# Six loads for a group's operand stacks instead of seven, two of them reading one block several times, and half of them moved behind another load in the queue

## The chip, the cores and the metric

The kernel runs on one core of a Trainium2 chip. The metric is device time in microseconds for one execution. TensorE does the matrix products, VectorE (DVE) and ScalarE (ACT) read their results, GpSimd (POOL) does small arithmetic on the side, and SyncE (SP) issues every DMA of this kernel, one after the other, as a queue written by hand. The data of a DMA are moved by 16 DMA engines that all transfers of the core share.

## The reference: what is computed

Cross attention with 32 heads of size 16 over four batches of 512 rows, and after it a feed-forward block with quantised activations and ternary weights. Cut to the part that the change touches:

```python
q = (layernorm(x) @ Wq).reshape(b, n, 32, 16)
k, v = jnp.split(ctx @ Wkv, 2, axis=-1)
q, k = apply_axial_rope(q, pos_map), apply_axial_rope(k, ctx_pos_map)
w = jax.nn.softmax(jnp.einsum("bqhd,bkhd->bhqk", q, k) / 4.0, axis=-1)
attn = jnp.einsum("bhqk,bkhd->bqhd", w, v).reshape(b, n, 512)
x = x + attn @ Wout + bout
x = x + ffn(layernorm(x), w_fc, w_proj)      # bitlinear, gelu, bitlinear
```

## The kernel before, in words

Three stages follow one another. In the first (to about 147 us) `Project` normalises, projects and rotates q and k, and splits each float32 value into three bf16 parts (0 is the coarse one, 2 the finest), which are stored in DRAM as `q_parts` and `k_parts`. In the second (147 to about 512 us) `Attend` works on 32 groups, each four heads of one batch. The third is the feed-forward block.

A product of q and k to nearly float32 precision is the sum of six products of parts. The kernel gets them in one matmul: it stacks six parts of q on 96 partitions (`q_stack`, six blocks of 16) and six parts of k on 96 partitions (`k_stack`), so that the contraction over 96 rows adds up six pairs. Each stack has four slots; group g uses slot g mod 4. `load_stacks` fills both from DRAM: a block of 16 partitions holds 4096 bytes in each, so a block is 64 KB, a stack 384 KB, and a group 768 KB.

TensorE's order is `tensor_step(s)`, for s = 2 to 34. Step s computes for group s the scores of which only the row maxima are kept (`scores`, L667, eight pairs of matmuls with `j` = 0 to 7, read by DVE at L740), for group s-2 the transposed scores less their maxima (`scores_turned`, L692, 16 matmuls, read by ACT's exponential at L760), and the product with v (`weigh_v`, L706). A step begins with one `scores_turned` matmul and then the first pair of `scores`. The maxima enter the transposed scores as two more rows of `q_stack` (98 rows in all), and they come there by a chain over engines: after the last L740 of a group, POOL negates and splits the maxima (`split_maxima`, L771 to L777), SP turns them with a DMA transpose (`turn_max`, L592), waits for that, and loads the result into the two rows (`load_max`, L596). So what is computed for group g in step g is used in step g+2, and one step lies between.

SP's order in iteration s of the attention loop, before:

```python
att.turn_max(sp, s - 2)       # waits for split_ready of group s-2
att.load_stacks(sp, s)        # 3 loads of q, 4 of k, for s = 4 to 31
att.load_max(sp, s - 2)       # waits for the turned maxima
att.load_weight(sp, w_fc, w_proj, s)
att.pack_sums(sp, s)          # store_sums; load_sums and store_inverse if s is even, load_quotients if odd
att.turn_weight(sp, s - 2)
```

`load_quotients` (odd s from 9 on) brings 256 KB of numerators (L638) and 256 KB of inverse sums (L639). Its source and its destination for each are these: 128 partitions of 2048 bytes in SBUF, and in DRAM a pattern whose outermost count is 8 heads with 16 rows inside (for the inverse sums the same row 16 times).

Of the kernel before, what the change touches and what calls it, by code (L numbers as in the profile page):

```python
# [15 lines left out]
BATCH, SEQ, DIM, CTX = 4, 512, 512, 256  # L16
HEADS, HEAD = 32, 16
# [4 lines left out]
GH = 4  # L22
HG = HEADS // GH
GROUPS = BATCH * HG
# [12 lines left out]
DMA = 16  # L37
PAIR_STORES = DMA * 2 * 2 * PARTS
STACK_SLOTS = 4
STACK_LOADS = DMA * 7  # L40
INPUT_SLOTS = 4
QUARTERS = FFN // DIM
O_SLOTS = 2
# [5 lines left out]
def need(eng, semaphore, value):  # L49

    if value > 0:
        eng.wait_ge(semaphore, value)
# [457 lines left out]
class Attend:  # L510
# [59 lines left out]

    def load_stacks(self, sp, g):
        mem, slot = self.mem, g % STACK_SLOTS
        for pair in range(2):
            sp.wait_ge(self.prj.parts_stored[pair], PAIR_STORES * (g // HG + 1))
        need(sp, self.st_ready, (g - STACK_SLOTS + 1) * 16)
        for stack_sb, where, runs in (
            (mem.q_stack, mem.q_parts, ((0, 0, 3), (3, 0, 2), (5, 0, 1))),
            (mem.k_stack, mem.k_parts, ((0, 1, 1), (1, 0, 1), (2, 0, 1), (3, 0, 3))),  # L580
        ):
            src = where[g].rearrange("t (d h) c -> (t d) (h c)", h=GH)
            for to, part, count in runs:
                sp.dma_start(stack_sb[to * HEAD:(to + count) * HEAD, slot].rearrange("p h c -> p (h c)"),  # L584
                             src[part * HEAD:(part + count) * HEAD]).then_inc(self.stacks_loaded[slot], DMA)

    def turn_max(self, sp, g):
        sp.wait_ge(self.split_ready, g + 1)
# [65 lines left out]
    def scores(self, pe, g, j):  # L654
        head, slot = j // 2, g % STACK_SLOTS
        if j == 0:
            pe.wait_ge(self.stacks_loaded[slot], (g // STACK_SLOTS + 1) * STACK_LOADS)
        if g == self.EARLY and j == 0:
# [13 lines left out]
    def early_scores(self, pe, i):  # L672

        g, head, c = i // (GH * CHUNKS), i // CHUNKS % GH, i % CHUNKS
        if i % (GH * CHUNKS) == 0:
            pe.wait_ge(self.stacks_loaded[g], STACK_LOADS)
        need(pe, self.early_read, i)
# [482 lines left out]
def xattn_ffn(nc, x, ctx, pos, wq, wkv, wout, bout, w_fc, w_proj, out):  # L1160
    with ExitStack() as stack:
# [3 lines left out]
        mem = Memory(nc, stack)  # L1165
        prj = Project(nc, mem, sem)
        att = Attend(nc, mem, prj, sem)
# [5 lines left out]
        @block.sync  # L1173
        def _(sp):
            prj.load_first(sp, x, ctx, pos, wq, wkv)
            prj.set_rows(sp, att.rows_set)
            prj.load_ctx(sp, ctx, 2)
            prj.load_x(sp, x, 2)
            for s in range(TILES + 6):
                if 3 <= s + 1 < TILES:  # L1180
                    prj.load_ctx(sp, ctx, s + 1)
                    prj.load_x(sp, x, s + 1)
                if within(s - 2, TILES):
                    prj.load_piece(sp, w_fc, w_proj, s - 2)
                if s == TILES + 4:
                    sp.wait_ge(prj.projected[1], TILES)
                    att.load_weight(sp, w_fc, w_proj, 0)
                    att.load_weight(sp, w_fc, w_proj, 1)
                if within(s - 5, TILES) and (s - 5) % 2 == 1:
                    prj.store_parts(sp, s - 5)  # L1190
                if s in (8, 10, 13, 15):
                    att.load_stacks(sp, (8, 10, 13, 15).index(s))
                if s == TILES + 3:
                    att.turn_max(sp, 0)
                    att.load_max(sp, 0)
            for pair in range(2):
                sp.wait_ge(prj.parts_stored[pair], PAIR_STORES * BATCH)

            for s in range(GROUPS + 3):
                if 1 <= s - 2 < GROUPS:  # L1200
                    att.turn_max(sp, s - 2)
                if STACK_SLOTS <= s < GROUPS:
                    att.load_stacks(sp, s)
                if 1 <= s - 2 < GROUPS:
                    att.load_max(sp, s - 2)
                if 2 <= s < GROUPS:
                    att.load_weight(sp, w_fc, w_proj, s)
                att.pack_sums(sp, s)
                if within(s - 2, GROUPS):
                    att.turn_weight(sp, s - 2)  # L1210
                if s == GROUPS - 7:
                    rows.load_bias(sp, bout)
                if GROUPS - 6 <= s < GROUPS - 2:
                    rows.load_weight(sp, wout, s - GROUPS + 6)
                if GROUPS - 2 <= s < GROUPS:
                    rows.load_x(sp, x, s - GROUPS + 2)
            rows.load_x(sp, x, 2)
            rows.turn_u(sp, 0)
            rows.load_x(sp, x, 3)
            rows.turn_u(sp, 1)  # L1220

            for s in range(TILES + 3):
                if s + 4 < TILES:
                    rows.load_x(sp, x, s + 4)
                if within(s - 1, TILES - 1):
                    rows.turn_h(sp, s - 1, 0)
                if s + 2 < TILES:
                    rows.turn_u(sp, s + 2)
                if within(s - 1, TILES - 1):
                    rows.turn_h(sp, s - 1, 1)  # L1230
                if s == TILES:
                    for part, half in ((0, 0), (0, 1), (1, 0), (1, 1)):
                        rows.turn_last(sp, part, half)
                if within(s - 3, TILES):
                    rows.store(sp, out, s - 3)
                if s < 6:
                    att.pack_sums(sp, GROUPS + 3 + s)
            for i in range(2):
                sp.wait_ge(rows.out_stored[i], TILES // 2 * DMA)
# [295 lines left out]
```

## Time and profile before

| | |
|---|---|
| time, median of 3 runs | 794.77 us (794.23 to 797.53) |
| the profiled execution's own time | 797.79 us |
| its span, first to last instruction | 795.9 us |
| PE busy | 768.5 us, 97% |
| DVE busy | 674.4 us, 85% |
| ACT busy | 456.1 us, 57% |
| DMA queue of SP, share of 16 engines | 65.7% |

The span leaves 1.9 us of the profiled execution outside the first and last instruction. PE is matmul, PEld the weight load that overlaps it, SPq is SP's own queue of DMA issues. A busy PE means that matmuls were in flight, not that TensorE was at its peak.

### The profile page before, as it was taken

To read this page: it belongs to the slowest core of one execution; us is meant where nothing else is said; L and a number is where in the kernel's file an instruction comes from. 1 tells how busy PE (TensorE), PEld (TensorE's weight loads), DVE (VectorE), ACT (ScalarE), POOL (GpSimd) and SP (SyncE) were. 2 spreads that over 40 slices of the span, in tenths; PEclk is the share of its full clock that TensorE was granted. 3 is DMA by queue.
4 is the path that set the end of the run, shared out by engine and by line. 5 is a ranking of instruction groups with operands and counts; after the bars stand their busy time and mean duration, and the time that the engine had idled before them with its cause. 6 is when DMAs were issued, how large, how long until landed. Compare 5 with 4: busy or idle time off the path is not lost.

```text
span 795.9 us, 11662 instructions
## 1 busy us (share of the span) xinstructions
PE 768.5 (97%) x3812; PEld 331.6 (42%) x3812; DVE 674.4 (85%) x945; ACT 456.1 (57%) x811; POOL 341.0 (43%) x445
## 2 busy tenths in 40 slices
PE   4899999799999999999999999999999999999998
PEld 3688877233333222323322222244444444444443
DVE  7788998688888888888888888269999999898895
ACT  5677776477777777767777777734322333223430
POOL 4688777743454455445445544623222121110001
PEclk9999999699999999999999999999999999999999
DMA  8488897535577769796887996326456654555545
GB/s 288 127 216 241 256 254 184 129 109 137 147 141 152 154 158 142 152 171 149 146 155 180 171 176 137 82 57 137 107 110 144 132 106 93 108 117 87 112 87 137
DMA packets 178861, 117.22 MB, mean 147 GB/s; under 512 B 119746, under 2 KB 150514, under 8 KB 178802
## 3 DMA queue, kind: packets, MB, share of 16 engines
q1 hardware_dynamic: 178802, 116.49, 65.7%
q8 instruction: 30, 0.49, 0.3%
q14 instruction: 29, 0.24, 0.1%
HBM read 64.50 MB, written 25.43 MB: 113 GB/s over the span
## 4 chain that ended last, share of the span: by engine, by line
PE 86%; DMA 6%; DVE 3%; SPq 2%; POOL 1%; issue 1%; ACT 1%; POOLq 0%; ACTq 0%
PE banks L967 14%; PE banks L952 14%; PE banks L706 13%; PE banks L692 12%; PE banks L281 11%; PE banks L667 11%; PE banks L938 7%; DMA stack_words<-max_rows 4%; DMA max_rows<-max_parts 2%; PE banks L310 2%; SPq L584 1%; PE banks L678 1%; DVE maxima L740 1%; DMA attn_words<-in_x_dram 1%; ACT probs_words L760 1%
## 5 line engine op out<-in xcount | busy, mean ns | idle before, releaser
L760 ACT ACTIVATE probs_words<-banks 128x512 f32<-128x512 f32 x512 | 272.1, 598 | 101.7 <-PE banks L692 101.0
L740 DVE TENSOR_REDUCE maxima<-banks 128x2 f32<-128x1024 f32 x240 | 283.4, 1216 | 45.6 <-PE banks L667 45.5
L692 PE MATMUL banks<-stack_words 98*128 98x512 bf16 x512 | 175.4, 386 | 4.8 <-DMA stack_words<-max_rows 3.4
L667 PE MATMUL banks<-stack_words 96*128 96x512 bf16 x480 | 144.9, 383 | 0.0
L706 PE MATMUL banks<-probs_words,late_words 128*32 128x512 f32 x1024 | 137.3, 608 | 0.7
L952 PE MATMUL banks<-ternary_words,late_words 128*128 128x512 f16 x512 | 113.1, 380 | 0.0
L967 PE MATMUL banks<-ternary_words,stack_words 128*128 128x512 f16 x512 | 112.9, 380 | 0.0
L1130 ACT ACTIVATE probs_words<-probs_words,h_moments 128x2048 f32<-128x2048 f32 (+1 forms) x17 | 32.2, 1901 | 135.4 <-DVE h_moments L1027 135.4
L692 PEld LDWEIGHTS banks<-stack_words 98*128 98x128 bf16 x512 | 39.8, 98 | 150.0 <-ACT probs_words L760 109.9
L771 POOL TENSOR_SCALAR neg_max<-maxima 128x16 f32<-128x16 f32 x32 | 8.3, 258 | 163.0 <-DVE maxima L740 161.2
L967 PEld LDWEIGHTS banks<-ternary_words,stack_words 128*128 128x128 f16 x512 | 49.9, 98 | 64.4 <-issue 6.6
L952 PEld LDWEIGHTS banks<-ternary_words,late_words 128*128 128x128 f16 x512 | 50.0, 98 | 61.5 <-issue 1.7
L1153 POOL TENSOR_SCALAR h_powers<-h_moments 128x1 f32<-128x1 f32 x16 | 5.5, 342 | 153.4 <-DVE h_moments L1027 153.4
L667 PEld LDWEIGHTS banks<-stack_words 96*128 96x128 bf16 x480 | 47.4, 99 | 56.7 <-issue 1.9
L1124 ACT ACTIVATE probs_words<-banks,row_scale 128x512 f32<-128x512 f32 x64 | 42.3, 682 | 27.5 <-PE banks L952 27.5
L938 PE MATMUL banks<-v_words,attn_words 128*128 128x512 f32 x128 | 57.7, 593 | 0.0
L786 POOL TENSOR_SCALAR late_words<-late_words,limits 128x512 f16<-128x512 f32 x32 | 50.1, 1566 | 0.3 <-POOL late_words L791 0.2
L788 POOL TENSOR_SCALAR late_words<-late_words,limits 128x512 f16<-128x512 f32 x32 | 50.2, 1570 | 0.0
L506 POOL TENSOR_TENSOR ternary_words<-attn_words,ternary_words 128x512 bf16<-128x512 f32 x32 | 37.3, 1166 | 24.3 <-ACT ternary_words L471 23.5
L706 PEld LDWEIGHTS banks<-probs_words,late_words 128*32 128x32 f32 x1024 | 20.2, 108 | 54.9 <-ACT probs_words L760 50.3
L502 POOL TENSOR_TENSOR attn_words<-attn_words 128x512 f32<-128x512 f32 x32 | 41.2, 1290 | 2.2 <-DVE attn_words L396 2.0
L1022 DVE BATCH_NORM_STATS2 h_stats<-probs_words 128x6 f32<-128x512 f32 x64 | 39.4, 679 | 0.0
(139 smaller groups left out, 962.5 us busy)
## 6 DMA issues: line engine op xcount, KB each, us to landing
o_rows<-late_words SPq DMA_DIRECT2D x32, 256.0 KB, 3.3
k_parts<-ternary_words SPq DMA_DIRECT2D x48, 128.0 KB, 3.2
q_parts<-ternary_words SPq DMA_DIRECT2D x48, 128.0 KB, 2.5
stack_words<-q_parts SPq DMA_DIRECT2D x32, 192.0 KB, 3.1
stack_words<-k_parts SPq DMA_DIRECT2D x96, 64.0 KB, 2.7
stack_words<-k_parts SPq DMA_DIRECT2D x32, 192.0 KB, 2.7
attn_words<-in_x_dram SPq DMA_DIRECT2D x16, 256.0 KB, 4.4
probs_words<-in_L_ffn_w_fc_dram SPq DMA_DIRECT2D x16, 256.0 KB, 3.7
```

The lines of the kernel that those rows point to most:

```text
L281: mm = self.nc.tensor.matmul(out, lhs[a][:, slot, k * P:(k + 1) * P], rhs[b][:, k, :], start=(a + b + k == 0), stop=(a == 1 and k == count ...
L667: mm = self.nc.tensor.matmul(self.score_slot[j % 2][:, i], self.mem.q_stack[0:STACK, slot, head, c * P:(c + 1) * P], self.mem.k_stack[0:ST ...
L692: self.nc.tensor.matmul(self.st_bank[(g * 16 + k) % self.ST_BANKS], self.mem.k_stack[0:STACK + 2, slot, head, c * P:(c + 1) * P], self.mem ...
L706: mm = self.nc.tensor.matmul(self.pv_bank[32 * j:32 * j + 32], self.v_ones[:, g % 2, c, j, :], self.probs[:, c, j, :], start=(c == 0), sto ...
L740: dve.tensor_reduce(self.maxima[:, g % 2, 2 * j:2 * j + 2], self.score_slot[j % 2], AX.X, ALU.max).then_inc(self.scores_read, 1)
L760: act.activation(self.probs[:, c, head, :], self.st_bank[(g * 16 + k) % self.ST_BANKS], ACT.Exp, scale=1 / math.sqrt(HEAD)).then_inc(self. ...
L786: pool.tensor_scalar(self.below[:], self.raw[:, w], limits[:, 1, w:w + 1], None, ALU.is_lt).then_inc(self.cut, 1)
L788: pool.tensor_scalar(self.ternary[:, w], self.raw[:, w], limits[:, 0, w:w + 1], None, ALU.is_gt).then_inc(self.cut, 1)
L938: mm = self.nc.tensor.matmul(self.y_bank[n % 2], att.attnT[:, n // CHUNKS * KX + k, c * P:(c + 1) * P], self.wout_sb[:, k, :], start=(k == ...
L952: mm = self.nc.tensor.matmul(self.fc_bank[o], self.uT[:, n % U_SLOTS, part * KX + k], self.fcT[:, k, o], start=(k + part == 0), stop=(k == ...
L967: mm = self.nc.tensor.matmul(self.proj_bank[r], self.hT[:, r, part, k], self.projT[:, k // 2, k % 2], start=(k + part == 0), stop=(part == ...
L1124: act.activation(self.h[:, n % H_SLOTS, o * DIM:(o + 1) * DIM], self.fc_bank[o], ACT.Gelu, scale=self.row_scale[:, n % U_SLOTS]).then_inc( ...
```

## The change

The six pairs of parts are the same six products in another order. The q stack holds parts 0,1,2,0,1,0 before and after. The k stack held 1,0,0,0,1,2 and holds 0,0,0,1,1,2 now. The four loads of k (three of one block, one of three blocks) become three: part 0 three times, part 1 twice, part 2 once. The first two read their one block of DRAM with an added outermost step of zero, counts 3 and 2, and write 48 and 32 partitions. In SP's attention loop the loads of q stay ahead of the load of the maxima, and those of k go behind it. The bytes moved are the same.

```diff
-STACK_LOADS = DMA * 7
+STACK_LOADS = DMA * 6
...
+    def load_q(self, sp, g):
...
+        src = self.mem.q_parts[g].rearrange("t (d h) c -> (t d) (h c)", h=GH)
+        for to, count in ((0, 3), (3, 2), (5, 1)):
+            sp.dma_start(self.mem.q_stack[to * HEAD:(to + count) * HEAD, slot].rearrange("p h c -> p (h c)"),
+                         src[0:count * HEAD]).then_inc(self.stacks_loaded[slot], DMA)
+
+    def load_k(self, sp, g):
+        slot = g % STACK_SLOTS
+        for part, to, count in ((0, 0, 3), (1, 3, 2), (2, 5, 1)):
+            src = self.mem.k_parts[g, part].rearrange("(d h) c -> d (h c)", h=GH)
+            sp.dma_start(self.mem.k_stack[to * HEAD:(to + count) * HEAD, slot].rearrange("p h c -> p (h c)"),
+                         src.unsqueeze(0).to_broadcast([count, HEAD, GH * SEQ])).then_inc(self.stacks_loaded[slot], DMA)
...
                 if STACK_SLOTS <= s < GROUPS:
-                    att.load_stacks(sp, s)
+                    att.load_q(sp, s)
                 if 1 <= s - 2 < GROUPS:
                     att.load_max(sp, s - 2)
+                if STACK_SLOTS <= s < GROUPS:
+                    att.load_k(sp, s)
```

SP's queue in one odd iteration of the attention loop, before: `max_rows` are the turned maxima, `max_parts` the maxima before it, `late_words` holds the raw weight, the quotients' operands and the ternary weight.

```order
L592 DMA_TRANSPOSE max_rows<-max_parts 128x128 [waits max_loaded_1,max_padded,split_ready]
L584 DMA stack_words<-q_parts 48x2048 [waits st_ready,parts_stored_1,parts_stored_0]
L584 DMA stack_words<-q_parts 32x2048
L584 DMA stack_words<-q_parts 16x2048
L584 DMA stack_words<-k_parts 16x2048 x3
L584 DMA stack_words<-k_parts 48x2048
L596 DMA stack_words<-max_rows 2x16x128 [waits max_turned_1]
L606 DMA late_words<-in_L_ffn_w_proj_dram 128x2x256 [waits ternary_ready]
L617 DMA o_rows<-late_words 128x512 [waits o_saved]
L638 DMA late_words<-o_rows 128x1x512 [waits inverse_stored_0]
L639 DMA late_words<-inverse_rows 128x1x512
L612 DMA_TRANSPOSE ternary_words<-late_words 128x4x128 [waits ternary_ready]
```

The same iteration of the changed kernel, in its own line numbers, from the maxima's transpose to the ternary weight's:

```order
L599 DMA_TRANSPOSE max_rows<-max_parts 128x128 [waits max_loaded_1,max_padded,split_ready]
L580 DMA stack_words<-q_parts 48x2048 [waits st_ready,parts_stored_1,parts_stored_0]
L580 DMA stack_words<-q_parts 32x2048
L580 DMA stack_words<-q_parts 16x2048
L603 DMA stack_words<-max_rows 2x16x128 [waits max_turned_1]
L587 DMA stack_words<-k_parts 48x1x2048
L587 DMA stack_words<-k_parts 32x1x2048
L587 DMA stack_words<-k_parts 16x2048
L613 DMA late_words<-in_L_ffn_w_proj_dram 128x2x256 [waits ternary_ready]
L624 DMA o_rows<-late_words 128x512 [waits o_saved]
L645 DMA late_words<-o_rows 128x1x512 [waits inverse_stored_0]
L646 DMA late_words<-inverse_rows 128x1x512
```

The load of the maxima moved ahead of four loads of k, and three loads of k now stand behind its wait; all that follows them (weights, sums, quotients) kept its order. The two broadcast loads have the same printed form as L638 and L639, a destination of partitions by one by a row. The order of TensorE, DVE, ACT and POOL is the same as before, instruction by instruction.

## Rows read from the trace of the kernel before

**Rows 1.** The page: span, granted clock by slice, and the chain that ended last.
```profile
span 795.9 us, 11662 instructions
...
PEclk9999999699999999999999999999999999999999
...
PE 86%; DMA 6%; DVE 3%; SPq 2%; POOL 1%; issue 1%; ACT 1%; POOLq 0%; ACTq 0%
```

**Rows 2.** Waits in the attention stage, 147 to 512 us: total, times, longest.
```profile
PEld banks L692 <- DMA stack_words<-max_rows: 7.8, 10, 1.6
...
PE banks L692 <- DMA stack_words<-max_rows: 3.4, 6, 1.1
...
SPq L592 <- POOL max_parts L777: 64.0, 30, 4.2
```

**Rows 3.** Chain that ended last, 296 to 335 us: start, duration, what.
```profile
298.25 0.45 PE banks L667 x2
...
298.72 1.24 DVE maxima L740
...
301.03 5.18 DMA max_rows<-max_parts
...
306.23 4.77 DMA stack_words<-max_rows
...
311.05 0.39 PE banks L692
```

**Rows 4.** Timeline of SP, 300 to 350 us: start, duration, issue.
```profile
302.30 1.44 SPq L584 DMA_DIRECT2D stack_words<-q_parts  x3
303.78 1.81 SPq L584 DMA_DIRECT2D stack_words<-k_parts  x4
306.23 0.71 SPq L596 DMA_DIRECT2D stack_words<-max_rows  x1
306.99 0.41 SPq L603 DMA_DIRECT2D late_words<-in_L_ffn_w_fc_dram  x1
...
324.92 1.12 SPq L592 DMA_TRANSPOSE max_rows<-max_parts  x1
...
336.27 1.12 SPq L592 DMA_TRANSPOSE max_rows<-max_parts  x1
```

**Rows 5.** Stretches of half a microsecond; the last two columns are DMA share and GB/s.
```profile
300.50:301.00 0.50, 0.50 (x7) 0.26 (x4) 0.50 (x2) 0.10 (x1) 0.42 (x3) 1.00 0.45 143
301.00:301.50 0.50, 0.50 (x4) 0.21 (x3) 0.50 (x2) 0.50 (x2) 0.50 (x2) 1.00 0.45 172
...
304.00:304.50 0.50, 0.50 (x4) 0.26 (x3) 0.11 (x1) 0.50 (x2) 0.42 (x2) 1.00 0.06 25
...
308.00:308.50 0.50, 0.50 (x9) 0.14 (x8) 0.50 (x2) 0.50 (x2) 0.00 (x0) 1.00 1.08 131
```

**Rows 6.** DMA issues of 301 to 312 us, an iteration of even s: KB each, us to landing.
```profile
stack_words<-q_parts SPq DMA_DIRECT2D x1, 192.0 KB, 5.0
stack_words<-k_parts SPq DMA_DIRECT2D x3, 64.0 KB, 5.3
...
ternary_words<-late_words SPq DMA_TRANSPOSE x1, 3.6
```

**Rows 7.** The same of 312.3 to 324 us, an iteration of odd s.
```profile
stack_words<-k_parts SPq DMA_DIRECT2D x3, 64.0 KB, 3.3
...
max_rows<-max_parts SPq DMA_TRANSPOSE x1, 2.2
...
ternary_words<-late_words SPq DMA_TRANSPOSE x1, 6.1
```

**Rows 8.** All that touches `stack_words`: duration min/median/max in ns, and its landings.
```profile
L584 SPq DMA_DIRECT2D stack_words<-k_parts x128: 407/420/1629, 63.6 to 479.4; - x128
...
DMA to landing us min/median/max: 2.1/3.2/5.5
```

**Rows 9.** Busy time in the attention stage; clock, DMA share and GB/s end the row.
```profile
147.00:500.00 353.00, 349.00 (x1937) 104.28 (x1938) 304.14 (x289) 258.51 (x486) 181.24 (x231) 0.99 0.72 148
```

More of the change, by code:

```diff
@@ L569, in __init__ @@
         self.divided = sem("divided")
-    def load_stacks(self, sp, g):
-        mem, slot = self.mem, g % STACK_SLOTS
+    def load_q(self, sp, g):
+        slot = g % STACK_SLOTS
         for pair in range(2):
@@ L577, in load_stacks @@
         need(sp, self.st_ready, (g - STACK_SLOTS + 1) * 16)
[L578 to L585, printed above, removed]
+        src = self.mem.q_parts[g].rearrange("t (d h) c -> (t d) (h c)", h=GH)
[3 more added lines that the diff above has]
+    def load_k(self, sp, g):
+        slot = g % STACK_SLOTS
+        for part, to, count in ((0, 0, 3), (1, 3, 2), (2, 5, 1)):
+            src = self.mem.k_parts[g, part].rearrange("(d h) c -> d (h c)", h=GH)
+            sp.dma_start(self.mem.k_stack[to * HEAD:(to + count) * HEAD, slot].rearrange("p h c -> p (h c)"),
+                         src.unsqueeze(0).to_broadcast([count, HEAD, GH * SEQ])).then_inc(self.stacks_loaded[slot], DMA)
+    def load_stacks(self, sp, g):
+        self.load_q(sp, g)
+        self.load_k(sp, g)
     def turn_max(self, sp, g):
```

## The prediction

> **What bounds the kernel now.** I read the page first, for its chain of work that ended last: 86% of it is TensorE, at a granted clock of nearly one throughout, and 6% is DMA [rows 1]. So the kernel is bound by TensorE, with small holes, and a change of DMAs can win at most those holes. Next the waits of the attention stage, to see how large they are: TensorE waited for the load of the maxima 7.8 us in its weight loads and 3.4 us in its matmuls, 11.2 us in all [rows 2]. It shows no wait for the q and k stacks. In the whole stage, TensorE was busy 349 of 353 us [rows 9]. SP is no bound: it waited 64 us for POOL's split maxima [rows 2].
>
> Then the chain in time, at one of the holes [rows 3]. The last matmuls of a step's scores end at 298.70. DVE and POOL take until 301.03, when SP issues the transpose of the maxima; it lands 5.18 us later, at 306.21. The load of the maxima is issued at 306.23, lands 4.77 us later, and TensorE goes on at 311.05. Steps without a hole are 11.35 us apart (336.27 - 324.92, [rows 4]). A chain therefore begins at the end of one step and is needed one step later. I call L its length, here 311.05 - 298.70 = 12.35 us. If L exceeds 11.35 us the excess is a hole, 1.0 us here. A hole also gives the next step's chain more room, because its chain started before the hole and its need comes after it. So over a pair of steps the holes add up to the excess of the slower of the two chains, not to the sum of both. Before: 14 pairs with 1.0 us are 14 us, against the 11.2 us seen, which bears the reckoning out.
>
> **The load of the maxima moved forward.** Before, it stood behind 3 + 4 stack issues of 1.44 + 1.81 us [rows 4], and its two partitions wait in the DMA engines behind all 768 KB of stacks. Four of those seven issues and half the bytes go behind it. In the step shown the issue was not late because of SP (the k issues ended at 305.59, the transpose landed at 306.21), but the landing was: 4.77 us for 8 KB. With 384 KB ahead instead of 768 KB, at the 131 GB/s at which the stack loads ran [rows 5], it lands 384/131 = 2.9 us sooner. L for the maxima falls to about 9.4 us, below 11.35. All 11.2 us of present holes go: -11.2 us. That is the gain, and its bound. The issue saved (0.42 us, [rows 8]) is worth nothing while SP waits 64 us for POOL.
>
> **The loads of k moved back.** They are issued after the maxima's load: at 306.99 instead of 303.78 in this step, since SP stands in its wait for the transpose. Behind them stand the weight load, the store of the sums, the quotients and the ternary transpose; all are slid back by 1.4 us or so, less than SP's average slack of 64/30 = 2.1 us, so I cost them at nothing. The k stack is needed at the second matmul group of the step, 0.22 us after its start. By [rows 6] the old k loads landed 5.3 us after issue, the last issue at about 305.1, so at 310.4, while the step could begin at 298.70 + 11.35 = 310.05 and wants the stack at 310.27. They had no room already, and the maxima's hole hid it: this cover is used up by the move.
>
> **The loads of k with a repeated block.** This term decides. The rows show one kind of transfer with a short outermost count, the quotients, whose count is 8. They are the last large transfers of an odd iteration, so I read the stretch just before the next transpose of maxima as theirs. There the DMA share stands at 0.45, which is 7.2 of 16 engines, at 143 to 172 GB/s, so 20 to 24 GB/s for each engine; and where the queue has nearly run dry one engine alone shows as a share of 0.06 with 25 GB/s [rows 5]. The stack loads of the other form reach all engines, a share of 1.08 [rows 5]. The ternary transpose, queued behind the quotients in odd iterations, landed in 6.1 us instead of 3.6 [rows 6, 7]. So a leading count of 8 gave 8 engines. I take it that leading counts of 3 and 2 give 3 and 2 engines. Then one engine carries 16 rows of 4096 bytes of the first load, 16 of the second and one of the third: 33 x 4096 = 135 KB, where it carried 6 x 4096 = 25 KB. At 25 GB/s that is 5.4 us, at 143/7.2 = 19.9 GB/s it is 6.8 us. To it comes the smallest landing of a stack load, 2.1 us [rows 8], which I take for what does not grow with size.
>
> The rows alone don't exclude that counts of 3 and 2 are spread in another way, by the 48 and 32 partitions of the destination, for instance. A rule of the Trainium skill bears on it, in DMA: Bandwidth & Descriptors, section "Why a DMA increments its semaphore by 16 and not by 1": the number of engines is the largest one, up to 16, that divides the slowest count above one of both sides; its "Rules for kernel authors" warn of just this leading broadcast. By the rule the sum is the one below; by a spread over all 16 it would be the first rival's. The trace agrees with the rule at the count of 8 and has no case of 3 or 2.
>
> **The sum.** L for the k stack in the changed kernel, from the end of a step's scores: 2.33 to the transpose's issue [rows 3]; the transpose's landing; 0.78 to the first k issue (0.02 + 0.71 + 0.05, [rows 4]); 2.1 fixed; the transfer; less 0.22, since it is needed that much after the step's start.
> The landing of the transpose is between 2.2 us [rows 7] and 5.18 us [rows 3]. It is 5.18 where the quotients still fill eight engines. Now the k loads add 4.7 us or so of work to two of these engines, while the hole gives them time to drain. I take 4.6, nearer the slow row.
> - Low: 2.33 + 2.2 + 0.78 + 2.1 + 5.4 - 0.22 = 12.6 us, excess 1.25 us a pair.
> - Taken: 2.33 + 4.6 + 0.78 + 2.1 + 5.4 - 0.22 = 15.0 us, excess 3.65 us a pair.
> - High: 2.33 + 5.18 + 0.78 + 2.1 + 6.8 - 0.22 = 17.0 us, excess 5.65 us a pair.
>
> Stacks are loaded in 28 iterations (s = 4 to 31), 14 pairs: 17, 51 and 79 us of holes. They replace the present 11.2: +6, +40, +68 us. The four groups that are loaded in the projection stage are loaded long before use; there I cost the crowding of two engines at nothing, since the inputs are loaded tiles ahead, with an upper bound of 4 x 2 = 8 us if such cover is gone. The feed-forward stage is the same and only starts later. Against the profiled execution (797.79 us, span 795.9) this gives 838 us; it stood 3.0 us above the median of 794.77, so against the median **835 us**, 5% slower.
>
> **Rivals.** *The repeated blocks are spread over all 16 engines* (the other side). For it: the rows have no count of 3 or 2, and the destination is 48 partitions. Against it: the share of 0.45 at a count of 8. Then the maxima's holes of 11.2 us go, but the k stack, whose data are issued 1.4 us or so later, lands between 310.4 as now and 311.1, that is 0.1 to 0.8 us late in every pair: 14 x 0.1 to 14 x 0.8 = 1 to 11 us of holes in place of 11.2. So 0 to -10 us, 785 to 795, about 790. It decides if the k loads land within 4 us of their issue. Chance 0.10, of which 0.07 is faster by over 0.5% (4 us, about what a measurement of this kernel can tell from no change).
>
> *Few engines, but the hole is covered.* If the transposes land in 2.2 us in all steps, and the narrow loads overlap with what is now waiting, the excess falls to the 0.8 us a pair that equals the present holes: about 795, within 0.5%. For it: 12.6 us is near 11.35. Against: three of the terms would have to be at or below their least row. Chance 0.06.
>
> *The two crowded engines become the bound.* Bytes of a pair of steps on the busiest engine: mean 148 GB/s x 22.7 us / 16 = 210 KB; 32 KB more because the quotients use half the engines; less 49 KB of old k, plus 270 KB of new: 463 KB. At 25 GB/s that takes 18.5 us and at 19.9 GB/s 23.3, under the forecast's pair of 26.4. From 17.5 GB/s down it decides. The stack loads ran at 131/16 = 8 GB/s for each engine when all ran at once [rows 5], so lower rates exist, though likely of something that all share. At 15 GB/s a pair is 30.9 us, 8.2 x 14 - 11 = +104 us: 899 us. Chance 0.06.
>
> **How the numbers follow.** The forecast has 0.78. Faster by over 0.5%: 0.07 (most of the first rival). Within 0.5%: 0.03 + 0.06 = 0.09. Slower: 0.78 + 0.06 = 0.84. The range reaches from the covered case (795, less 2 for what runs differ by) to the high sum (794.77 + 68 = 863) with the projection's bound (8), 3 more because the pairs are alike only roughly: 793 to 874. It leaves out most of the first rival and the third, about 0.16. The forecast's own range is 801 to 863.
>
> **What would show it.** If right: TensorE's wait for the maxima is gone; a new wait stands at the first scores of a step (before L667's matmuls) for k's loads, 2 to 6 us in every second step or shared between both; k's loads of 192 KB and 128 KB land in 7 us and more, and stretches with a DMA share of 0.12 to 0.2 at 50 to 75 GB/s appear. If wrong: k's loads land in 2 to 4 us. TensorE's clock was at 1.00 where the present holes are; a fall with the longer holes would add to the time, and is in no term. Most of the error I expect in the landing of the transpose, behind two crowded engines.

## The result, and the profile after

The changed kernel takes 881.78 us (median of 6 runs, 877.27 to 883.33), the kernel before 796.85 us in the same count of runs (794.23 to 798.62). The ratio is 1.106, with a 95% interval of 1.103 to 1.110: some 85 us slower, where 835 us was forecast and 874 us was the upper end of the range. All numbers below are of the faster of the chip's two states; one execution of one experiment (896.12 us, the kernel with small quotients and no fillers) fell in the slower state and is left out.

First the page of the changed kernel: span, granted clock by slice, and the chain that ended last.

```profile
span 880.0 us, 11630 instructions
...
PEclk9999998999999899978999788999999999999999
...
PE 66%; DMA 15%; SPq 9%; DVE 4%; issue 2%; POOL 2%; ACT 1%; POOLq 0%; DVEq 0%; ACTq 0%
```

Against [rows 1] the span has grown by 84.1 us, TensorE's share of the chain has fallen from 86% to 66%, DMA's has risen from 6% to 15%, and the clock shows sevens and eights in the middle, where the attention stage lies. Where the time went is told by the waits of that stage (147 to 600 us; total, times, longest), which answer to [rows 2]:

```profile
PEld banks L674 <- DMA stack_words<-k_parts: 55.6, 16, 4.2
PE banks L674 <- DMA stack_words<-k_parts: 47.7, 15, 3.7
...
PE banks L699 <- DMA stack_words<-max_rows: 1.1, 1, 1.1
```

L674 is the `scores` matmul (L667 before), L699 the transposed one (L692 before). The wait for the maxima is gone but for one; a wait for k of about 3.2 us stands at 15 steps, one in each of the 14 pairs and one more behind the last. It shows twice, once for the weight load and once for the matmul behind it: these are the same holes. The chain in time through one of them answers to [rows 3]:

```profile
332.98 0.45 PE banks L674 x2
...
333.45 1.24 DVE maxima L747
...
338.47 0.74 SPq L603
...
339.25 0.74 SPq L587
...
340.69 7.80 DMA stack_words<-k_parts
...
348.54 0.99 PE banks L674 x2
```

From the end of the scores (333.43) to the landing of k (348.49) it is 15.06 us. The first k load is issued at 339.25 and all of k has landed 9.24 us later; before, a k load of such an iteration landed 5.3 us after its issue [rows 6]. The timeline of SP, which answers to [rows 4], gives the length of a pair of steps:

```profile
335.77 1.11 SPq L599 DMA_TRANSPOSE max_rows<-max_parts  x1
...
347.11 1.11 SPq L599 DMA_TRANSPOSE max_rows<-max_parts  x1
...
363.78 1.11 SPq L599 DMA_TRANSPOSE max_rows<-max_parts  x1
```

One step is 11.34 us as ever, the other 16.67: the pair takes 28.01 us. Stretches of half a microsecond around the hole (TensorE first, clock, DMA share and GB/s last), to set beside [rows 5]:

```profile
346.00:346.50 0.50, 0.00 (x0) 0.00 (x0) 0.02 (x1) 0.00 (x0) 0.26 (x1) 1.00 0.18 74
...
347.50:348.00 0.50, 0.00 (x0) 0.00 (x0) 0.00 (x0) 0.00 (x0) 0.50 (x1) 1.00 0.13 49
...
349.00:349.50 0.50, 0.50 (x3) 0.05 (x1) 0.00 (x0) 0.00 (x0) 0.50 (x1) 0.50 0.25 26
...
351.50:352.00 0.50, 0.50 (x5) 0.13 (x2) 0.04 (x1) 0.00 (x0) 0.08 (x1) 0.50 0.95 131
352.00:352.50 0.50, 0.50 (x3) 0.20 (x2) 0.50 (x1) 0.19 (x1) 0.32 (x1) 0.96 0.67 131
```

Two things are to be seen. While TensorE waits, the DMA share is 0.18 at 74 GB/s and then 0.13 at 49 GB/s: three engines of sixteen, then two, each at about 25 GB/s. (Of the other five half microseconds of this hole one has 0.20 at 66 GB/s. In the other four, with shares of 0.80 to 5.88, other transfers are mixed in.) And from the end of the hole to 352 us TensorE runs at 0.50, its 1.2 GHz level. In the trace before, the clock was at 1.00 from 156 to 500 us, its holes included.

The attention stage as a whole, from its first transposed scores to the first matmul of the next stage, before and after (TensorE's busy time is the first number behind the length):

```profile
147.57:505.53 357.96, 353.38 (x1961) 105.02 (x1962) 304.07 (x288) 262.66 (x495) 186.36 (x235) 0.99 0.72 148
```

```profile
152.93:589.67 436.74, 386.79 (x1961) 107.77 (x1962) 307.55 (x288) 264.26 (x495) 186.93 (x235) 0.91 0.76 122
```

The stage grew by 78.8 us. TensorE took 33.4 us longer over the same matmuls, at a mean clock of 0.91 instead of 0.99, and stood idle for 45.4 us more.

### The profile page after: what moved, and what is told of

Same layout as the page of the kernel before. It is cut to its first block, busy times and chain, and to the rows that moved or that the text cites. A ratio compares the mean times of both kernels' runs of the same rounds, so it can differ in the third digit from the quotient of the medians.

```text
span 880.0 us, 11630 instructions
## 1 busy us (share of the span) xinstructions
PE 803.5 (91%) x3812; PEld 335.8 (38%) x3812; DVE 678.9 (77%) x945; ACT 457.5 (52%) x811; POOL 340.8 (39%) x445
## 4 chain that ended last, share of the span: by engine, by line
PE 66%; DMA 15%; SPq 9%; DVE 4%; issue 2%; POOL 2%; ACT 1%; POOLq 0%; DVEq 0%; ACTq 0%
PE banks L974 13%; PE banks L959 13%; DMA stack_words<-k_parts 12%; PE banks L713 10%; PE banks L699 8%; PE banks L674 8%; PE banks L281 7%; PE banks L945 6%; SPq L587 2%; DVE maxima L747 2%; SPq L580 2%; SPq L599 2%; PE banks L310 1%; SPq L603 1%; SPq L243 1%
## 5 line engine op out<-in xcount | busy, mean ns | idle before, releaser
L674 PE MATMUL banks<-stack_words 96*128 96x512 bf16 x480 | 155.1, 406 | 47.7 <-DMA stack_words<-k_parts 47.7
L699 PE MATMUL banks<-stack_words 98*128 98x512 bf16 x512 | 184.8, 405 | 2.5 <-ACT probs_words L767 1.3
L713 PE MATMUL banks<-probs_words,late_words 128*32 128x512 f32 x1024 | 150.9, 664 | 0.7
L699 PEld LDWEIGHTS banks<-stack_words 98*128 98x128 bf16 x512 | 41.1, 100 | 161.7 <-ACT probs_words L767 98.4
L674 PEld LDWEIGHTS banks<-stack_words 96*128 96x128 bf16 x480 | 48.0, 103 | 115.2 <-DMA stack_words<-k_parts 55.6
```

What stands on the lines that cost most here:

```text
L674: mm = self.nc.tensor.matmul(self.score_slot[j % 2][:, i], self.mem.q_stack[0:STACK, slot, head, c * P:(c + 1) * P], self.mem.k_stack[0:ST ...
L699: self.nc.tensor.matmul(self.st_bank[(g * 16 + k) % self.ST_BANKS], self.mem.k_stack[0:STACK + 2, slot, head, c * P:(c + 1) * P], self.mem ...
L713: mm = self.nc.tensor.matmul(self.pv_bank[32 * j:32 * j + 32], self.v_ones[:, g % 2, c, j, :], self.probs[:, c, j, :], start=(c == 0), sto ...
```

## The experiments

Times are medians with the ratio to the kernel before, run on the same chip, and its 95% interval.

**The place in the queue alone.** Seven loads of the old form, k behind the maxima.

```diff
-STACK_LOADS = DMA * 6
+STACK_LOADS = DMA * 7
...
+        src = self.mem.k_parts[g].rearrange("t (d h) c -> (t d) (h c)", h=GH)
+        for to, part, count in ((0, 1, 1), (1, 0, 1), (2, 0, 1), (3, 0, 3)):
+            sp.dma_start(self.mem.k_stack[to * HEAD:(to + count) * HEAD, slot].rearrange("p h c -> p (h c)"),
+                         src[part * HEAD:(part + count) * HEAD]).then_inc(self.stacks_loaded[slot], DMA)
```

> Only the place in the queue is changed: seven loads of the old form (every one on a source of 16 or 48 rows), q ahead of the maxima's load, k behind it. Theory (the broadcast loads sit on 3 and 2 of the 16 DMA engines, and all of the loss comes from that): no hole over 1 us at a step's start, TensorE's clock stays at about 0.99, and the time is that of the kernel before or a few us less: 786 to 798 us. Rival (the place behind the maxima's load, 3.2 us later, makes k late): a wait for k_parts in every second step as in the changed kernel, 3 us or more, and 840 to 885 us.

797.17 us, ratio 1.001 (0.9985 to 1.0035): no change. Its waits show why there was no gain either:

```profile
PE banks L674 <- DMA stack_words<-k_parts: 1.1, 2, 0.6
...
PE banks L699 <- DMA stack_words<-max_rows: 0.3, 1, 0.3
```

The maxima are hardly waited for any more, and what is left is a short wait for k. So with loads of the old form the move is harmless and worth nothing that can be measured; the loss is not from the place alone.

**The form alone.** Six loads with the leading broadcasts, all ahead of the maxima's load.

```diff
-                    att.load_q(sp, s)
+                    att.load_stacks(sp, s)
...
-                if STACK_SLOTS <= s < GROUPS:
-                    att.load_k(sp, s)
```

> Only the form is changed: six loads with the two leading broadcasts, all ahead of the maxima's load as before. Theory (narrow loads are the cost): the chain now ends with the maxima's load, which waits on the same crowded engines behind k; L is shorter than in the changed kernel because k is issued about 3 us earlier, so holes of 2 to 5 us a pair: 830 to 885 us. Rival (the place is the cost, the form costs nothing): 790 to 800 us.

869.08 us, ratio 1.090 (1.0855 to 1.0951). The form alone carries 72 us of the loss. The place, which costs nothing with the old form, adds some 13 us to the narrow one. The wait has changed its name, since the maxima's two rows now queue behind the narrow loads:

```profile
PE banks L699 <- DMA stack_words<-max_rows: 40.7, 14, 3.5
```

**The same repetition with an outermost count of 16.** Rows of a block are interleaved in the stacks, for q and k alike, so that the copies are the inner count.

```diff
-        src = self.mem.q_parts[g].rearrange("t (d h) c -> (t d) (h c)", h=GH)
+        src = self.mem.q_parts[g].rearrange("t (d h) c -> d t (h c)", h=GH)
...
-                         src[0:count * HEAD])
+                         src[:, 0:count])
...
-                         src.unsqueeze(0).to_broadcast([count, HEAD, GH * SEQ]))
+                         src.unsqueeze(1).to_broadcast([HEAD, count, GH * SEQ]))
```

> Queue order and number of loads (six) as in the changed kernel, same bytes; the rows of a block are interleaved in the stacks (partition d x count + copy), so that the outermost count of every source is 16 and the repetition is the inner one. The six products are the same. Theory (outermost count sets the number of engines): k lands in 2.5 to 4.5 us, no holes over 1 us, clock about 0.99, 785 to 797 us. Rival (reading one block of DRAM several times, or the step of zero itself, is slow): as the changed kernel, 860 to 885 us.

801.37 us, ratio 1.005 (1.0028 to 1.0074). The same bytes from the same blocks with the same step of zero, in the same order and number of loads, lose 4 us instead of 85. Issues of its stretch 301 to 313 us (KB, us to landing):

```profile
stack_words<-k_parts SPq DMA_DIRECT2D x1, 192.0 KB, 3.3
...
stack_words<-k_parts SPq DMA_DIRECT2D x1, 128.0 KB, 3.2
```

So it is the outermost count, not the reading of one block three times. The time lies 4 us above the theory's band: this kernel still waits 7.5 us for k, in nine steps. The cured form thus gains nothing over the kernel before either.

**Half the dose.** Part 0 in three loads of 16 rows; only part 1 keeps its leading broadcast of 2. The busiest engine has 20 rows a group instead of 33.

```diff
-STACK_LOADS = DMA * 6
+STACK_LOADS = DMA * 8
...
-        for part, to, count in ((0, 0, 3), (1, 3, 2), (2, 5, 1)):
+        for part, to, count in ((0, 0, 1), (0, 1, 1), (0, 2, 1), (1, 3, 2), (2, 5, 1)):
```

> The changed kernel with part 0 of k in three loads of 64 KB (16 rows each, outermost count 16) in place of one with a leading broadcast of 3; part 1 keeps its leading broadcast of 2. The busiest engine has 3 + 16 + 1 = 20 rows of k a group instead of 33. Theory (time follows the rows on the busiest engine, 5.3 us a pair of steps for 27 rows more than before's 6): 14 rows more than before's 6 give about half of the loss, 835 to 850 us. Rival (only the broadcast of 3 matters, or the number of issues): 795 to 805 us or 875 to 885 us.

838.55 us, ratio 1.054 (1.050 to 1.057), +43 us. For 14 rows more than before on the busiest engine that is 3.1 us a row; the changed kernel has 27 rows more and 85 us, 3.1 us a row too. At these two doses the loss is in proportion to the rows on the busiest engine, inside the theory's band. Its parts are not: in the attention stage TensorE's matmuls took 11.3 us longer than before (33.4 in the changed kernel) and its idle time grew by 26.1 us (45.4). So the straight line is a sum of two parts that bend, and no law to go by at other doses.

**Keeping TensorE busy in the hole.** Twelve extra matmuls, whose results are overwritten, fill part of the hole.

```diff
+        if j == 0 and g >= 6 and g % 2 == 0:
+            need(pe, self.scores_read, (g - self.EARLY) * 2 * GH - 1)
+            for i in range(12):
+                self.nc.tensor.matmul(self.score_slot[0][:, i % 2], ...)
         if j == 0:
             pe.wait_ge(self.stacks_loaded[slot], (g // STACK_SLOTS + 1) * STACK_LOADS)
```

> The changed kernel with 12 more matmuls (96 rows x 512 columns, 2.6 us at the full clock, results overwritten) on TensorE ahead of its wait for the stacks, in the 13 steps of even s from 6 on, where its holes are. Theory (each hole of 3.5 us is followed by 3.4 us at a granted clock of 0.5, which costs 1.7 us more): the holes that are left are under 1.5 us, the clock in the attention stage is 0.99 or so, and the time falls by 13 x 1.7 = 22 us or a little more, to 852 to 862 us, though more work is done. Rival (the clock in these stretches costs nothing, since TensorE waits anyway): 880 us or more.

878.57 us, ratio 1.100 (1.095 to 1.104), with a mean clock of 0.977 instead of 0.948. The time fell by 3 us, not by 22. In the attention stage the clock rose from 0.91 to 0.97. TensorE was busy 399.55 of 434.27 us there, of which the 13 groups of fillers are 13 x 2.75 = 36 us, so its own matmuls took 10 us longer than before the change instead of 33: the clock did give back some 23 us. But fillers and idle time together are 70.5 us, where the changed kernel idled for 50, and that took 20 of the 23 us away again. Part of it shows in the chain:

```profile
334.30 4.05 DMA max_rows<-max_parts
...
361.98 5.37 DMA max_rows<-max_parts
```

The maxima's transpose now lands in 4.1 and 5.4 us, where the changed kernel's load of the maxima could be issued 2.70 and 2.88 us after it (median landing of all 32 transposes: 4.0 us against 2.7). In the changed kernel 16.67 us lie between the transpose of the odd iteration and the next one, here 14.98, so the engines have less time to drain. That this is why the transpose is slower is argued, not shown.

**The quotients taken off the crowded engines**, with the fillers and without them. Both kernels leave out most of the numerators and inverse sums.

```diff
+        if pair < 2:
             sp.dma_start(self.numer[:, r], rows[0]).then_inc(self.inverse_loaded[r], DMA)
...
+        else:
+            for now in (self.numer, self.inverse):
+                sp.dma_start(now[0:HEAD, r], rows[0][0]).then_inc(self.inverse_loaded[r], DMA)
```

> The kernel with the 12 filling matmuls in even steps, and with the two quotient loads of every pair of groups from the third on cut from 256 KB (8 engines, 64 KB on each) to 32 KB (16 rows); it leaves out the numerators and inverse sums of those pairs. With the fillers the transpose of the maxima landed in 4.1 to 5.4 us and ate up what the clock gave back. Theory (the backlog of the two crowded engines, to which the quotients belong, sets that landing): it falls to under 3 us, a pair of steps to about 26 us, and the time by some 12 x 2 = 24 us, to 850 to 860 us. Rival (the two narrow k loads alone set the pair, whatever else is queued): 875 us or more.

> The changed kernel without fillers, with the quotient loads cut in the same way; it leaves out the same data. In the changed kernel the transpose ahead of the long hole already lands in under 3 us, since a hole and a slow stretch give the engines time to drain. Theory (the chain of an even step, 2.3 us to the transpose, 2.7 for it, 0.8, and 9.2 for k, sets the pair together with the half clock after the hole): little changes, 870 to 882 us. Rival (the sum of all work on the busiest engine sets the pair): 64 KB less at 25 GB/s is 2.6 us a pair, 845 to 858 us.

With fillers 868.97 us, ratio 1.092 (1.087 to 1.096): 10 us less than with the fillers alone by the medians, 6 by the ratios, and not 24. It lies between the two bands. Without them 870.41 us (median of three runs, 869.61 to 880.22), ratio 1.097 (1.091 to 1.103): 11 us less than the changed kernel by the medians, 7 by the ratios, at the lower edge of the theory's band. The backlog of the quotients is thus a part, but the smaller one: with it gone and the clock mostly kept, most of the loss is still there, and k still lands 8 us after its last issue.

The kernel without fillers shows something else, from 181 to 233 us. It has a hole in every step there, not one in each pair:

```profile
181.21 0.60 PE L678 MATMUL banks<-stack_words 96*128 96x512 bf16 x2 [1.61 <-DMA stack_words<-k_parts]
...
194.13 0.60 PE L678 MATMUL banks<-stack_words 96*128 96x512 bf16 x2 [1.41 <-DMA stack_words<-k_parts]
...
207.46 0.61 PE L678 MATMUL banks<-stack_words 96*128 96x512 bf16 x2 [1.81 <-DMA stack_words<-k_parts]
```

The granted clock stays at 1.00 (from 175 to 245 us), and a pair of steps takes 26.3 us. Later in the same trace, with one hole of 3.0 to 3.3 us in each pair and a slow stretch behind it, a pair takes 27.5 us (345.93 to 373.38).

**A hole without any DMA.** The base is a kernel with hardly any holes (the next experiment, 795.06 us). ACT runs small instructions behind the first exponential of every second step, and TensorE waits for them.

```diff
+        if j == 0 and g >= 6 and g % 2 == 0:
+            pe.wait_ge(self.pause_over, (g // 2 - 2) * 8)
...
+            for i in range(8):
+                need(act, self.pause_over, (g // 2 - 2) * 8 + i)
+                act.activation(self.prj.ones[:], self.mem.ident[:], ACT.Exp).then_inc(self.pause_over, 1)
```

> The kernel with k split around the maxima's load, which has no holes, and with a pause made without DMAs: in the 13 steps of even s from 6 on, TensorE waits before the first scores for 8 small ACT instructions (128x128, about 0.4 us each) behind the first exponential of the step, so some 3.5 us. Theory (a hole of 3.5 us is followed by 3.4 us at a granted clock of 0.5, and that costs 1.7 us more): clock 0.96, time 795 + 13 x (3.5 + 1.7) = 862 us. Rival (the clock fell in the changed kernel for another reason): clock 0.98 or more, 795 + 13 x 3.5 = 841 us.

> The same with 3 small ACT instructions, a pause of some 1.5 us. Theory (short holes, as those of 1 us before, leave the clock alone): clock 0.985 or more, 795 + 13 x 1.5 = 815 us. Rival (any hole costs clock): clock under 0.975, 825 us or more.

Eight instructions: 865.57 us, ratio 1.086 (1.082 to 1.089), clock 0.953. Three: 825.27 us, ratio 1.036 (1.033 to 1.039), clock 0.979. The waits of the two (the profile calls their releaser "issue"), long one first:

```profile
PE banks L678 <- issue: 44.5, 13, 3.4
```

```profile
PE banks L678 <- issue: 22.4, 13, 1.7
```

Against the base the long pauses cost 70.5 us, of which 44.5 are the holes and 26.0 lie behind them: 2.0 us a hole. (The base ran on another chip, where the kernel before took 1.5 us less; that much of the 26.0 may be the chip.) The traces agree: in the attention stage TensorE's matmuls took 382.1 us here and 353.1 in the base, 29.0 us longer. In the stretches of this kernel after one hole the clock stood at half from 314 to 321 us:

```profile
314.50:315.00 0.50, 0.41 (x2) 0.17 (x3) 0.00 (x0) 0.00 (x0) 0.50 (x2) 0.50 0.25 56
...
320.00:320.50 0.50, 0.50 (x3) 0.23 (x2) 0.50 (x1) 0.33 (x1) 0.00 (x0) 0.50 0.92 272
320.50:321.00 0.50, 0.50 (x3) 0.01 (x1) 0.47 (x1) 0.27 (x1) 0.00 (x0) 0.69 0.89 299
```

The short pauses cost 30.2 us, of which 7.8 are not the holes, 0.6 us each; here too stretches at 0.50 follow (302 to 305 us). The theory for the long pauses held, clock and time. That short ones leave the clock alone did not hold: 825 us is the rival's mark, and the clock lies between the two.

**k split around the maxima.** Old form, seven loads: q (3), k (192 and 64 KB), maxima, k (64 and 64 KB).

```diff
+    K_FIRST, K_LAST = ((3, 0, 3), (0, 1, 1)), ((1, 0, 1), (2, 0, 1))
...
                     att.load_q(sp, s)
+                    att.load_k(sp, s, att.K_FIRST)
                 if 1 <= s - 2 < GROUPS:
                     att.load_max(sp, s - 2)
                 if STACK_SLOTS <= s < GROUPS:
-                    att.load_k(sp, s)
+                    att.load_k(sp, s, att.K_LAST)
```

> The kernel with seven loads of the old form, but the maxima's load stands between the four loads of k: q (3), k (192 and 64 KB), maxima, k (64 and 64 KB). SP issues two k loads in the 2.4 us in which it waited for the transpose. Theory (with the maxima moved forward the last load of k is late by 0.5 to 1 us in its place, and both ends can be met): no hole over 0.5 us, 787 to 793 us. Rival (the maxima's load or k is as late as before): 794 to 798 us.

795.06 us (12 runs), ratio 0.9993 (0.9974 to 1.0013). The holes did go:

```profile
PE banks L675 <- DMA stack_words<-k_parts: 0.7, 3, 0.3
```

but there was only that much in them: the matmuls' own idle time before was 3.4 us [rows 2], 0.4% of the time, which this measurement can't tell from none. The time lies in the rival's band. It is the best version here, and a tie with the kernel before.

**The projection stage alone.** The kernel before, with the broadcasts only in the first four groups' loads.

```diff
+            if g < STACK_SLOTS and where is mem.k_parts:
+                continue
...
                     att.load_stacks(sp, (8, 10, 13, 15).index(s))
+                    att.load_k_early(sp, (8, 10, 13, 15).index(s))
```

> The kernel before, with the leading broadcasts of k (counts 3 and 2) only in the loads of the first four groups, in the projection stage, one load less each; the attention stage is that of before. Theory (crowding two engines there holds up the loads of x and ctx: in the changed kernel the attention stage began at 152.9 instead of 147.6 us): 4 to 6 us slower, 799 to 803 us. Rival (the inputs are loaded far enough ahead, the 5.3 us came from elsewhere): 793 to 798 us.

804.59 us, ratio 1.0107 (1.0079 to 1.0135), +7.4 us for four groups, 1.6 us above the theory's band. Waits of this kernel from 26 to 153 us:

```profile
ACT attn_words L477 <- DMA probs_words<-in_L_ffn_w_proj_dram: 8.9, 2, 4.6
...
PEld banks L686 <- DMA stack_words<-k_parts: 3.8, 1, 3.8
...
DVE project_stats L381 <- DMA attn_words<-in_x_dram: 3.4, 1, 3.4
```

None of these waits stands in the same stretch of the kernel before. The weight, k and x landed too late, though the inputs are loaded tiles ahead: x took 9.2 us to land in the median of this stage, against 4.0 before, and ctx 9.0 against 2.7.

## Why the prediction was right and where it was wrong

*The form sets the number of engines.* Right, and shown for the counts 3 and 2: a share of 0.18 at 74 GB/s and 0.13 at 49 GB/s is three and two engines at 25 GB/s, as forecast from the count of 8 in [rows 5]; and the interleaved kernel takes the loss away with nothing but another outermost count. The first rival (spread over 16) is out.

*The length of the chain.* 15.06 us from the end of the scores to the landing in the step shown, against 15.2 forecast (15.0 with the 0.22 us by which it is needed later). The total is right by two errors that cancel. The transpose was costed at 4.6 us and let the maxima's load go after 2.70 us, perhaps since hole and slow stretch gave the engines time. The k loads were costed at 2.1 + 5.4 = 7.5 us and took 9.24 us from the first issue. The 33 rows at 25 GB/s account for 5.4 of it; q's rows ahead on the same engines and the three issues for the rest, I suppose, and no run splits that.

*Holes.* 51 us forecast for 14 pairs, 47.7 us seen in 15 steps. The rule that a pair has one hole held in the changed kernel, but the one with small quotients had a hole of 1.3 to 1.8 us in every step from 181 to 233 us, so the rule does not always hold.

*The present holes, -11.2 us.* Wrong by counting the same holes twice: 7.8 us of the weight loads' wait and 3.4 us of the matmuls' are two views of one wait, as the 55.6 and 47.7 us of the changed kernel make plain. What there was to win is nearer to 3.4 us, and the two reordered kernels of the old form won nothing measurable. With it falls the check of the reckoning, "14 us, against the 11.2 us seen": the holes seen are 3.4 us in 6 steps, so most pairs before had none.

*The clock, "in no term".* This is the step that failed. The prediction saw the possibility of a fall and priced it at nothing, because the clock was at 1.00 at holes of 1 us. The rows of the stage show what it cost: TensorE's matmuls took 386.79 us instead of 353.38, 33.4 us longer. With the 45.4 us of added idle time that is the whole 78.8 us by which the stage grew. That the holes themselves bring the slow clock is shown without any DMA: 13 pauses of 3.4 us cost 26 us more than their own length by the medians, 29 by the traces.

*That the slow clock can simply be taken away again* is, however, not what the fillers show: some 23 us of clock came back, and 3 us of time. The pair of steps was then 27.7 us (11.35 + 2.33 + 4.05 + 0.78 + 9.12, from 334.30 on), with a transpose of 4.05 us where the changed kernel had 2.70. So take the slow clock away, and longer waits for DMAs fill most of the pair. The third rival (two engines as the bound) does not hold as it was put: it wanted 17.5 GB/s or less for each engine, and about 25 were seen, at which its bytes take 18.5 us of the pair. The small quotients took 64 KB a pair off each crowded engine and freed only 6 to 11 us of the 85, and all engines stand idle for moments within the pair (a DMA share of 0.00 from 341.0 to 341.5 us). What exactly holds the pair near 28 us, beyond the k loads' own length, stays open.

*The projection stage at nothing.* Wrong: 5.3 us in the trace (the attention stage began at 152.93 us, not 147.57) and 7.4 us in the experiment, near the bound of 8 us that was given for a cover gone. The cover of inputs loaded tiles ahead was not enough.

So of the 44 us between the 838 forecast for the profiled execution and its 882, 33 are the clock's, 5 more idle time in the attention stage (8 for the double count, less 3 since the holes were shorter than forecast), and 5 the projection stage. The other 3 of the 47 us between 835 and 882 come from the way to a median: the forecast was carried down by 3.0 us, but the changed kernel's profiled execution lay at its median.

## What to carry to other kernels

- A repeated block in one DMA should not have the repetition as its outermost count: put a count of 16 outermost and interleave the destination to suit. Here the two forms differ by 80 us for the same bytes, and even the good one won nothing over seven plain loads. The rule of the Trainium skill, DMA: Bandwidth & Descriptors, "Why a DMA increments its semaphore by 16 and not by 1", gives 3 and 2 engines for these loads. The trace agrees, with shares of 0.18 at 74 GB/s and 0.13 at 49 GB/s.
- When a forecast says that TensorE will stand still for several microseconds in each of many steps, price the slow stretch behind it as well: here 2.0 to 2.4 us for a hole of some 3.3. Before and after, compare TensorE's busy time for the same matmuls: what it grew by is the clock's part.
- The same hole stands in the list of waits once for the weight load and once for the matmul. Take the matmul's.

## What the runs showed of the hardware that was not expected

- The granted clock fell to 0.50 behind pauses of 1.7 us too: 13 of them brought the mean clock from 0.989 to 0.979 and cost 7.8 us beyond themselves (or 6.3, if the 1.5 us between the chips is taken off). But it stayed at 1.00 behind five holes of 1.3 to 1.8 us in a row in the kernel with small quotients. No run here shows what tells the two cases apart.
- Behind holes of over 3 us the slow stretch was not of one length: in the changed kernel 3.5 us (348.5 to 352) behind one hole and 10 us (376 to 386) behind the next, in the kernel with long pauses 7 us (314 to 321).
- The kernel's time grew by 3.1 us for each row of 4096 bytes on the busiest DMA engine, for 14 rows as for 27, though neither the holes nor the clock's part grew in that proportion.
- Four early groups with narrow loads were enough to make 256 KB loads of x land in 9.2 us instead of 4.0.
